# Twelve bf16 products of constants per chunk in the recurrence of a four-layer kernel

## The chip, the cores and the metric

The kernel runs on one core of one Trainium2 chip. The metric is the device time of one execution in microseconds (us). Lower is better.

## The reference, cut to what matters

The reference is a network of four layers, each an attention-like part plus a feed-forward part. The part that matters here is the attention of the first layer: a recurrence over time in which a memory matrix M is updated by each token and then normalised over all its entries.

```python
def step(M, kv):
    k_t, v_t = kv
    v_pred = jnp.einsum('bf,bfd->bd', k_t, M)
    surprise = jnp.linalg.norm(v_t - v_pred, axis=-1, keepdims=True)
    delta = k_t[:, :, None] * v_t[:, None, :]
    M = M + eta_c[None, :, None] * surprise[:, :, None] * delta
    return (_ln2(M), None)
M, _ = jax.lax.scan(step, M0, (kT, vT))
```

`_ln2` subtracts the mean of M and divides by its standard deviation. As the kernel lays it out there are 16 sequences of 256 tokens. The recurrence is serial in time: the scalar weight of each token depends on the state after the token before.

## The kernel before, in words

All engines have instruction streams written out by hand, and semaphores tie them together. The kernel is a row of stages with a barrier after each. The recurrence is the fourth stage. It works in chunks of C = 8 tokens; NC = 32 chunks, numbered c = 0 to 31.

Within a chunk the eight tokens are stepped through on VectorE (DVE) and ScalarE (ACT) alone, with small vectors: two square roots a step on ACT and some seven small operations on DVE. TensorE (PE) works at the border of two chunks and in the background. Its order for one chunk c is fixed by `scan_pe`:

- **The head.** Products of the new weights `vw` and `wc` with the masked key products of `cross_pe` (into PSUM banks 1 and 2); then, each waiting for a DVE addition (`sc_pT`), the product of `pT0` with the values (bank 5), the second part of `pT1`, four one-column sums (bank 3), and the product of `pT1` (bank 6). Then `rescale_pe`, whose result ACT copies (`sc_rc`) before it scales five of the eight blocks of the state (`scaled_act`), and only then takes the first square root of the chunk. Then PE waits for `sc_ex` and makes the **spreading product** `K("blk")` times `ex` (bank 7), from which DVE starts the steps.
- **The update.** `update_pe` makes 16 products with 32 rows each, `sums_pe` adds the scaled state through the identity in four pairs, waiting for ACT's scaling (`sc_scl`).
- **The keys.** `cross_pe` makes two products for chunk c + 2, of 256 columns each.
- **The state's products with the next keys.** Eight products of a block of the state with 16 tokens each (32 columns, fp32) into bank 4, in four pairs. Each pair waits for ACT's copy of two new blocks (`sc_new`), and ACT makes one copy in each of the steps 3 to 6. After them the next chunk's head waits for `vw` (`sc_vw`).

PE runs its stream strictly in order. A product of fp32 operands appears in the trace as two MATMUL records, one of bf16 operands as one. Every matrix product is recorded at the one line of the helper `mm`, L204; the tiles tell them apart:

- `ps<-big,tmp`, `ps<-big,sm`, `ps<-big,mw`: the head's wide products
- `ps<-co,mw` and `ps<-sm,co`: the one-column sums, and the rescaling product (8 columns)
- `ps<-mw,co` with 96 columns: the spreading product
- `ps<-tmp,big` and `ps<-sm,mw` with 32 rows: the update
- `ps<-big,co`: `sums_pe`
- `ps<-ke` and `ps<-ke,co`: `cross_pe`
- `ps<-ke,big` with 32 columns: the state's products with the next keys

On ACT, `sm<-ps 128x8` is the copy behind the rescaling product, `big<-big,co,sm` is `scaled_act`, `big<-ps 128x256` is the copy of new state blocks (and of bank 4 for the next chunk), and `sm<-sm 128x1` is a square root.

Of the kernel before, what the change touches and what calls it, by code (L numbers as in the profile page):

```python
# [12 lines left out]
BF16 = mybir.dt.bfloat16  # L13
# [119 lines left out]
def program(nc, xT, early, wts, bia, con, m1, m2, m3, outT):  # L133
    with ExitStack() as ctx:
# [13 lines left out]
        def signals(engine, *counts):  # L148
            out = []
            for n in counts:  # L150
                s, base = idle[engine].pop(0) if idle[engine] else (sem(f"{engine}_{next(made)}"), 0)
                out.append(Signal(s, base))
                held.append((engine, s, base + n))
            return out
# [16 lines left out]
        PS = ctx.enter_context(nc.psum_tensor("ps", [128, 8, 512], F32))  # L171

        def W(n, a=0, b=None):
            if n in EAT:
                o, w = EAT[n]
                return MW[:, 2048 + o + a:2048 + o + (w if b is None else b)]
            o, w = WAT[n]
            return WT[:, o + a:o + (w if b is None else b)]
# [5 lines left out]
        def K(n, a=0, b=None):  # L184
            if n in EAT:
                return W(n, a, b)
            o, w = CAT[n]
            return CO[:, o + a:o + (w if b is None else b)]
# [3 lines left out]
        def small(n):  # L192
            a = smat[0]
            smat[0] += n
            assert smat[0] <= 680
            return SM[:, a:a + n]
# [6 lines left out]
        def mm(e, out, lhsT, rhs, start=True, stop=True):  # L203
            return e.matmul(out, lhsT, rhs, start=start, stop=stop)  # L204
# [341 lines left out]
        def cv(buf, c):  # L546
            return buf[:, 128 * c:128 * c + 128]
# [163 lines left out]
        def tables_sp(e):  # L711
# [25 lines left out]
        C2 = small(16).rearrange("p (t x) -> p t x", x=2)  # L737
        one8r = small(8)
        rp8, Rc, Wst, tmp8 = small(8), small(8), small(8), small(8)
        corr = PS[:, 4, 0:256].rearrange("p (k n) -> p k n", k=2)  # L740
        ORDER = (0, 2, 4, 6, 1, 3, 5, 7)
        s_rt = [sem(f"d_rt{i}") for i in range(RTB)]
# [2 lines left out]
        sc_cross, sc_next, sc_p0, sc_p0e, sc_p1, sc_p2, sc_p3, sc_exp, sc_rc, sc_up, sc_sum = signals(  # L745
            "tensor", 31, 30, 31, 31, 31, 31, 31, 31, 32, 256, 124)
# [6 lines left out]
        def tok(c, a=0, b=128):  # L753
            return KE[:, :, 128 * c + a:128 * c + b]

        def cross_pe(e, c):
            if c > 1:
                e.wait_ge(*sc_xm(c - 1))
            mm(e, PS[:, 0, 0:256], cv(EK, c - 1), tok(c))
            mm(e, PS[:, 0, 256:512], K("one"), tok(c)).then_inc(sc_cross.sem, 1)  # L760
# [4 lines left out]
        def rescale_pe(e, c):  # L765
            e.wait_ge(*sc_rp(c))
            mm(e, PS[:, 4, 256:264], K("rselA"), rp8).then_inc(sc_rc.sem, 1)

        def update_pe(e, c):
            if c > 1:  # L770
                e.wait_ge(*sc_new(4 * (c - 1)))
            e.wait_ge(*sc_vwr(c))
            if c == 1:
                e.wait_ge(s_ek, 16 * 32)
            for mean in range(2):
                for a in ORDER:

                    r32 = slice(32 * (a // 2), 32 * (a // 2) + 32)
                    if mean:
                        mm(e, moved(a), K("hm", 128 * (a % 2), 128 * (a % 2) + 128)[r32, :], wcr[r32, :].broadcast_to((32, 128)),  # L780
                           start=False, stop=(c == NC and a % 2 == 1)).then_inc(sc_up.sem, 1)
                    else:
                        mm(e, moved(a), EK4[c - 1][r32, a % 2, :], vwr[r32, :], start=(a % 2 == 0), stop=False)

        def sums_pe(e, c):

            for k in range(4):
                e.wait_ge(*sc_scl(8 * (c - 1) + 2 * k + 2))
                mm(e, PS[:, (2, 3, 5, 6)[k], 0:256], K("ident"), U[:, 256 * k:256 * k + 256], start=False, stop=True).then_inc(sc_sum.sem, 1)

        def scan_pe(e):
            cross_pe(e, 1)
            for c in range(NC):
                if c:
                    e.wait_ge(*sc_vw(c))
                    e.wait_ge(*sc_xm(c))
                    mm(e, PS[:, 1, 0:128], vw, XMK[c % 2][:, 0:128], start=True, stop=False)
                    e.wait_ge(*sc_wc(c))
                    mm(e, PS[:, 1, 0:128], wc.broadcast_to((128, 128)), XMK[c % 2][:, 256:384], start=False, stop=True).then_inc(sc_p0.sem, 1)
                    mm(e, PS[:, 2, 256:384], vw, XMK[c % 2][:, 128:256], start=True, stop=False)  # L800
                    e.wait_ge(*sc_pT(2 * c - 1))
                    mm(e, PS[:, 5, 0:128], pT0, cv(VT, c)).then_inc(sc_p1.sem, 1)
                    mm(e, PS[:, 2, 256:384], wc.broadcast_to((128, 128)), XMK[c % 2][:, 384:512], start=False, stop=True).then_inc(sc_p0e.sem, 1)
                    mm(e, PS[:, 3, 257:258], pT0, K("one")[:, 0:1])
                    e.wait_ge(*sc_sq(c))
                    mm(e, PS[:, 3, 256:257], sqp, K("one")[:, 0:1]).then_inc(sc_p2.sem, 1)
                    e.wait_ge(*sc_pT(2 * c))
                    mm(e, PS[:, 6, 0:128], pT1, cv(VT, c)).then_inc(sc_p3.sem, 1)
                    rescale_pe(e, c)
                    e.wait_ge(*sc_ex(c))  # L810
                    mm(e, PS[:, 7, 0:96], K("blk"), ex).then_inc(sc_exp.sem, 1)
                    update_pe(e, c)
                    sums_pe(e, c)
                if c + 2 < NC:
                    cross_pe(e, c + 2)
                if c and c + 1 < NC:
                    for a in range(8):
                        if a % 2 == 0:
                            e.wait_ge(*sc_new(4 * (c - 1) + a // 2 + 1))
                        p = mm(e, corr[:, :, 16 * a:16 * a + 16], Mst[:, a, :], tok(c + 1, 16 * a, 16 * a + 16), start=(a == 0), stop=(a == 7))  # L820
                    p.then_inc(sc_next.sem, 1)
            rescale_pe(e, NC)
            update_pe(e, NC)

# [1985 lines left out]
        def _(e):  # L2810
# [7 lines left out]
            first_pe(e)  # L2818
            barrier(e, st.up())
            scan_pe(e)  # L2820
            barrier(e, st.up())
            mo_pe(e)
# [302 lines left out]
```

## Time and profile before

| | |
|---|---|
| median of 3 runs | 2213.94 us (2213.69 to 2222.31) |
| span of the profiled execution | 2256.3 us |
| PE busy | 1912.8 us (85%) |
| DVE busy | 1357.7 us (60%) |
| ACT busy | 1044.8 us (46%) |
| mean granted TensorE clock | 0.821 |
| recurrence's chunks in the trace | from 242 to 770 us |

The time is that of executions without the profiler; the span is from the first to the last instruction of one profiled execution, and no separate time is given for that one. In the profile, the granted clock is 1.00 at TensorE's full 2.4 GHz and 0.50 at 1.2 GHz. PE's busy time is high partly because a slow clock stretches its products. The columns of a timeline are: start, duration from the first start to the last end of a merged group, engine, line, operation, tiles, shape, count, and idle time before it with its releaser.

### The profile page before, as it was taken

The page shows a single profiled execution, that of the slowest core. Times are in us where ns is not written, and L with a number is a line of the kernel's source. Part 1 is how long each engine was busy: PE and PEld are TensorE (multiplying, and loading weights), DVE is VectorE, ACT ScalarE, POOL GpSimd, SP SyncE. Part 2 cuts the span into 40 slices and gives each one's busy share as a digit, 9 for nine tenths or more (in the row PEclk, how much of TensorE's full clock was granted, in tenths as well). Part 3 has the DMA queues.
Part 4 walks back from the last instruction along what each step waited for, and adds up shares of the span by engine and source line. Part 5 has one row for each costly group of instructions (what it writes and reads, how often), then busy time and mean ns, then how long its engine had stood idle before and what let it go on. Part 6 is the DMA issues. An engine that isn't in the chain of part 4 may idle for free.

```text
span 2256.3 us, 35340 instructions
## 1 busy us (share of the span) xinstructions
PE 1912.8 (85%) x12022; PEld 1293.6 (57%) x12022; DVE 1357.7 (60%) x4960; ACT 1044.8 (46%) x2490; POOL 319.3 (14%) x455
## 2 busy tenths in 40 slices
PE   6887777787778799999999888888899954999888
PEld 4464566666666566886555776555454542973333
DVE  3777888888888644676333485542121431569886
ACT  2433555665566423333444223454344313437667
POOL 0001000000000000330000002003126023406642
PEclk9999666667676568898999657998999967988989
DMA  2001100000000000000001100003013200635662
GB/s 111 1 13 36 32 22 22 19 19 25 19 19 19 34 1 1 2 3 2 0 1 75 40 1 1 1 15 97 13 12 50 89 14 30 113 69 91 98 103 40
DMA packets 93282, 76.09 MB, mean 34 GB/s; under 512 B 22320, under 2 KB 85168, under 8 KB 92336
## 3 DMA queue, kind: packets, MB, share of 16 engines
q1 hardware_dynamic: 85424, 65.31, 12.8%
q0 software_dynamic: 7680, 8.53, 2.0%
q8 instruction: 97, 1.59, 0.3%
q14 instruction: 81, 0.66, 0.1%
HBM read 48.86 MB, written 23.51 MB: 32 GB/s over the span
## 4 chain that ended last, share of the span: by engine, by line
PE 56%; DVE 23%; ACT 6%; DMA 4%; issue 4%; SPq 3%; another core or an unknown queue 1%; POOL 1%; DVEq 0%; PEld 0%; PEldq 0%; ACTq 0%; POOLq 0%
PE ps L204 52%; DVE sm L225 8%; ACT big L213 3%; DVE mw L225 3%; DMA d_pt<-big 3%; DVE big L217 2%; PE ps L208 2%; PE ps L2465 2%; SPq L2552 1%; DVE big L231 1%; DVE tmp L221 1%; ACT sm L213 1%; SPq L866 1%; DVE big L225 1%
## 5 line engine op out<-in xcount | busy, mean ns | idle before, releaser
L213 ACT ACTIVATE tmp<-ps,bi 128x512 f32<-128x512 f32 (+1 forms) x226 | 153.9, 684 | 200.8 <-PE ps L204 189.3
L204 PE MATMUL ps<-big,mw 128*128 128x512 f32 (+3 forms) x476 | 236.3, 593 | 11.6 <-DVEq L252 5.6
L213 ACT ACTIVATE sm<-sm 128x1 f32<-128x1 f32 x512 | 174.4, 341 | 106.6 <-DVE sm L225 96.0
L204 PE MATMUL ps<-ke,big 32*128 32x128 f32 (+2 forms) x1632 | 154.0, 296 | 62.3 <-ACT big L212 61.8
L204 PE MATMUL ps<-big,co 128*128 128x256 f32 (+1 forms) x360 | 180.5, 636 | 27.9 <-DMA bi<-bia 12.2
L213 ACT ACTIVATE big<-ps,co 128x512 f32<-128x512 f32 (+1 forms) x296 | 174.5, 648 | 61.3 <-PE ps L204 58.2
L204 PEld LDWEIGHTS ps<-ke,big 32*128 32x128 f32 (+2 forms) x1632 | 132.3, 195 | 87.4 <-ACT big L212 72.0
L231 DVE TENSOR_REDUCE big<-ps 128x2 f32<-128x512 f32 x256 | 161.2, 675 | 21.0 <-PE ps L204 20.7
L204 PE MATMUL ps<-ke 48*128 48x256 bf16 (+4 forms) x638 | 127.5, 315 | 34.7 <-DVE big L217 16.7
L204 PE MATMUL ps<-big,tmp 128*32 128x256 f32 (+2 forms) x1180 | 137.5, 424 | 22.9 <-DVE tmp L221 17.6
L217 POOL TENSOR_TENSOR big<-big,co 128x512 f32<-128x512 f32 x32 | 40.1, 1274 | 765.6 <-ACT big L212 765.6
L204 PE MATMUL ps<-tmp,mw 128*128 128x512 f32 x288 | 140.9, 601 | 0.7 <-ACT tmp L212 0.7
L204 PE MATMUL ps<-big 128*32 128x128 f32 (+5 forms) x898 | 130.1, 299 | 10.3 <-DMA big<-big 5.1
L204 PE MATMUL ps<-big,wt 128*128 128x512 f32 x208 | 114.5, 653 | 24.8 <-DVEq L252 14.4
L204 PEld LDWEIGHTS ps<-big,co 128*128 128x128 f32 x360 | 88.9, 276 | 75.8 <-issue 27.1
L204 PEld LDWEIGHTS ps<-co,sm 128*128 128x128 f32 (+1 forms) x708 | 95.2, 208 | 64.4 <-DVE sm L333 37.6
L212 ACT ACTIVATE big<-ps 128x256 f32<-128x256 f32 (+4 forms) x244 | 90.7, 381 | 89.2 <-PE ps L204 72.6
L204 PEld LDWEIGHTS ps<-big,mw 128*128 128x128 f32 (+1 forms) x476 | 93.0, 229 | 66.5 <-issue 36.8
L204 PE MATMUL ps<-co,sm 128*128 128x128 f32 (+1 forms) x708 | 109.1, 304 | 22.6 <-DVE sm L333 12.6
L204 PEld LDWEIGHTS ps<-ke 128*128 128x128 f32 (+3 forms) x638 | 65.9, 133 | 92.4 <-DVE big L217 23.5
L225 DVE SCALAR_TENSOR_TENSOR sm<-sm,mw 128x1 f32<-128x1 f32 (+1 forms) x480 | 101.0, 221 | 23.3 <-ACT sm L213 13.0
L204 PE MATMUL ps<-tmp,wt 128*128 128x512 f32 (+1 forms) x212 | 102.5, 574 | 11.6 <-issue 5.8
(254 smaller groups left out, 3834.5 us busy)
## 6 DMA issues: line engine op xcount, KB each, us to landing
mw<-d_tab SPq DMA_DIRECT2D x32, 328.0 KB, 3.4
mw<-m SPq DMA_DIRECT2D x2, 4096.0 KB, 12.7
d_pt<-big SPq DMA_DIRECT2D x32, 192.0 KB
ke<-d_pt SPq DMA_DIRECT2D x72, 64.0 KB
big<-d_pt SPq DMA_DIRECT2D x72, 64.0 KB
mw<-d_pt SPq DMA_DIRECT2D x48, 64.0 KB
d_xs<-big SPq DMA_DIRECT2D x1, 2560.0 KB, 15.3
big<-d_xs SPq DMA_DIRECT2D x5, 512.0 KB, 6.4
```

The lines of the kernel that those rows point to most:

```text
L204: return e.matmul(out, lhsT, rhs, start=start, stop=stop)
L208: return e.transpose(out, a, K("ident")[0:n, 0:n])
L212: return e.activation(out, in_, f, scale=scale, **kw)
L213: return e.activation(out, in_, f, bias=K("zero")[0:out.shape[0], :] if bias is None else bias, scale=scale, **kw)
L217: return e.tensor_tensor(out, a, b, op)
L221: return e.tensor_scalar(out, a, s1, None, op0)
L225: return e.scalar_tensor_tensor(out=out, in0=a, scalar=s, in1=b, op0=op0, op1=op1)
L231: return e.tensor_reduce(out, a, AX, op)
L866: e.dma_start(BIG[2 + hh][q, :].rearrange("p (c x) -> p c x", x=256)[:, :, 64 * (b % 4):64 * (b % 4) + 64], EKT[q, 16 * hh:16 * hh + 16, : ...
L2465: p = e.matmul(o, TMP[:, 2 + i % 2, 128 * j:128 * j + 128], MW[:, bass.ds(x * 512 + (4096 + 128 * j), 128)], start=False, stop=(j == 3))
L2552: e.dma_start(st_[j][r0 + 8 * t:r0 + 8 * t + 8], d_pt[n, j, part].rearrange("(h d) n -> d h n", d=8)).then_inc(s_st[n % 4], 16)
```

## The change

PE gets products of two constants, 128 rows by 128 columns of weights and 384 moving columns, in bf16 (a bit view of the constant table `colr`). Their results go to columns 128 to 511 of PSUM bank 1, which nobody reads. `heat_pe(e, n)` makes n of them. Two stand after the rescaling product, ahead of the wait for `sc_ex` and the spreading product, in chunks 1 to 31. Ten stand among the state's products with the next keys, in chunks 1 to 30: three behind each of the first three pairs, one behind the last. The signal `sc_next` is given by the last state product, as before, ahead of the one added product.

```diff
+        heat_w, heat_x = K("colr", 0, 64).bitcast(BF16), K("colr", 0, 192).bitcast(BF16)
...
+        def heat_pe(e, n):
+            for _ in range(n):
+                mm(e, PS[:, 1, 128:512], heat_w, heat_x)
...
                     rescale_pe(e, c)
+                    heat_pe(e, 2)
                     e.wait_ge(*sc_ex(c))
                     mm(e, PS[:, 7, 0:96], K("blk"), ex).then_inc(sc_exp.sem, 1)
...
                         p = mm(e, corr[:, :, 16 * a:16 * a + 16], Mst[:, a, :], tok(c + 1, 16 * a, 16 * a + 16), start=(a == 0), stop=(a == 7))
-                    p.then_inc(sc_next.sem, 1)
+                        if a == 7:
+                            p.then_inc(sc_next.sem, 1)
+                        if a % 2:
+                            heat_pe(e, 1 if a == 7 else 3)
```

## Rows read from the trace of the kernel before

**Rows 1.** The page, part 2: 40 equal slices of the span, in tenths.
```profile
PEclk9999666667676568898999657998999967988989
```

**Rows 2.** Windows: the recurrence, then the head of chunk 2 and later stretches.
```profile
core 0: us, PE busy (x) PEld busy (x) DVE busy (x) ACT busy (x) POOL busy (x), PEclk, DMA share, GB/s
242.00:770.00 528.00, 418.65 (x2436) 346.19 (x2436) 454.18 (x2749) 319.18 (x949) 0.00 (x0) 0.67 0.06 19
250.80:254.60 3.80, 2.60 (x18) 2.23 (x18) 3.56 (x25) 1.21 (x4) 0.00 (x0) 1.00 0.30 91
492.60:497.00 4.40, 4.34 (x18) 3.99 (x18) 3.45 (x22) 0.79 (x3) 0.00 (x0) 0.50 0.23 76
497.70:503.80 6.10, 5.99 (x41) 4.51 (x42) 5.42 (x32) 4.87 (x15) 0.00 (x0) 0.50 0.00 1
506.00:510.00 4.00, 1.89 (x12) 1.56 (x12) 3.40 (x24) 2.65 (x10) 0.00 (x0) 1.00 0.00 0
```

**Rows 3.** Waits of PE from 267 to 752 us: in total, times, longest, us.
```profile
PE ps L204 <- ACT big L212: 60.1, 85, 0.8
...
PE ps L204 <- ACT big L213: 6.2, 10, 1.0
```

**Rows 4.** The chain in order of time, heads of chunks 3 and 16: start, us, what.
```profile
267.03 4.34 PE ps L204 x18
...
492.64 4.35 PE ps L204 x18
497.02 0.19 ACT sm L212
497.23 2.04 ACT big L213 x5
```

**Rows 5.** Timeline of PE, chunk 2: first and last product of its head, and behind.
```profile
250.83 0.49 PE L204 MATMUL ps<-big,tmp 128*128 128x128 f32 x2 [0.37 <-DVE tmp L221]
...
253.69 0.29 PE L204 MATMUL ps<-sm,co 128*128 128x8 f32 x2
254.95 0.74 PE L204 MATMUL ps<-mw,co 128*128 128x96 f32 x2 [0.97 <-DVE mw L217]
```

**Rows 6.** Timeline of ACT, heads of chunks 2 and 16.
```profile
254.01 0.18 ACT L212 ACTIVATE sm<-ps 128x8 f32<-128x8 f32 x1 [1.47 <-PE ps L204]
...
256.16 0.28 ACT L213 ACTIVATE sm<-sm 128x1 f32<-128x1 f32 x1
...
499.17 0.28 ACT L213 ACTIVATE sm<-sm 128x1 f32<-128x1 f32 x1
```

**Rows 7.** Timeline of PE, the last head (chunk 31); of ACT, its first square root.
```profile
752.36 0.79 PE L204 MATMUL ps<-big,tmp 128*128 128x128 f32 x2
...
757.47 0.74 PE L204 MATMUL ps<-mw,co 128*128 128x96 f32 x2 [0.78 <-DVE mw L217]
...
758.88 0.28 ACT L213 ACTIVATE sm<-sm 128x1 f32<-128x1 f32 x1
```

**Rows 8.** Timeline of PE, the last layers: bf16 products of 256 columns and their neighbours.
```profile
1414.60 1.87 PE L204 MATMUL ps<-ke 128*128 128x256 bf16 x8
1416.26 1.91 PE L204 MATMUL ps<-co,sm 128*128 128x128 f32 x8
...
1419.10 1.03 PE L204 MATMUL ps<-ke 128*128 128x256 bf16 x8
1420.01 1.16 PE L204 MATMUL ps<-co,sm 128*128 128x128 f32 x8
```

**Rows 9.** Timeline of PEld and PE, the state's products with the next keys.
```profile
490.12 0.89 PEld L204 LDWEIGHTS ps<-ke,big 128*128 128x128 f32 x4 [0.88 <-ACT big L212]
...
508.92 0.52 PEld L204 LDWEIGHTS ps<-ke,big 128*128 128x128 f32 x4 [0.88 <-ACT big L212]
...
508.93 0.63 PE L204 MATMUL ps<-ke,big 128*128 128x32 f32 x4 [0.77 <-ACT big L212]
510.04 0.49 PE L204 MATMUL ps<-big,tmp 128*128 128x128 f32 x2 [0.48 <-DVE tmp L221]
```

## Prediction

> **What bounds the kernel now.** I read the page first, then windows over the recurrence, then PE's waits, then the chain and the timelines of single chunks. In the page the reader should look at the line of the granted clock: full in the first slices, then 0.6 to 0.7 for the ten slices of the recurrence [rows 1]. The windows give that stretch as 528 us, a quarter of the span, at a mean clock of 0.67 [rows 2]. DVE is busy 454 us of it and PE 419, but neither is full: the chunk is one serial chain that changes engines. What matters is where PE stands on this chain, and at which clock.
>
> PE is off the chain while the eight tokens are stepped. It then waits for ACT's copies, 85 times for 60.1 us in all, and no wait is longer than 1.0 us [rows 3]. During the state's products with the next keys it is busy 1.89 of 4.00 us, at the full clock; behind that stretch the clock falls, and the head of chunk 16, where PE is busy 4.34 of 4.40 us, runs at 0.50 [rows 2]. So does the stretch after it (5.99 of 6.10 us), and the clock comes back only then. PE is slow where the chain goes through it, and fast where it waits.
>
> In the head PE is on the chain: 4.35 us of products in chunk 16, then ACT's copy of the rescaling factors, 2.04 us of scaling, and the first square root [rows 4]. The scaling on ACT, not the spreading product, ends last there, so what counts is how early the rescaling product comes.
>
> **What a head is worth at the full clock.** The trace has the case once. The head of chunk 2 ran at 1.00 up to its spreading product [rows 2]. From its first product (250.83) to the end of the rescaling product (253.69 and 0.29) it took 3.15 us, against 4.35 us in chunk 16; ACT's copy came at 254.01, 3.18 us after the first product, against 4.38 (492.64 to 497.02); the first square root at 256.16, 5.33 against 6.53 (492.64 to 499.17) [rows 4, 5, 6]. So a head at the full clock is 1.20 us shorter. The whole chunk confirms it: 250.83 to 267.03 is 16.20 us. The next 28, from 267.03 to 752.36 [rows 4, 7], take 485.33 us, 17.33 each. Some of these already have the first products of the head at full clock, which is why the mean is 17.33 and not 17.40.
>
> If every head ran like that of chunk 2: 28 x 16.20 = 453.6, so 31.7 us less; and the head of chunk 31, from 752.36 to its square root at 758.88, is 6.52 us instead of 5.33 [rows 6, 7], 1.2 us more. Sum 32.9 us. The head of chunk 1 gains nothing, since the update behind it waited for a transfer.
>
> **What the added products cost.** No row has one of 384 columns. The nearest are bf16 products of 128 rows and 256 columns: eight take 0.91 us at the full clock (1419.10 to 1420.01), 0.114 each, and eight take 1.66 us at, nearly all, half of it (1414.60 to 1416.26), 0.21 each [rows 8]. Times 1.5: 0.17 and 0.31 us each. Per chunk that is 2.0 us or 3.7 us of PE. Whether it costs anything depends on the waits:
>
> - Between the state's products. The waits of some 0.77 us lie between pairs 1.40 us apart, one for each step. At full clock a pair keeps the array's loads busy 0.52 us [rows 9], and three added products 0.51: 1.03 of 1.40 us, hidden. The last pair starts 1.11 us ahead of the next head (508.93 to 510.04 [rows 9]): 0.52 + 0.17 leaves 0.4 us. Cost 0. The cover is gone at half clock: 0.89 + 0.93 = 1.82 of 1.40 us, and the fourth pair then ends with 3 x 1.82 + 0.89 + 0.31 = 6.66 us after the first began, where the head is due after 4.20 + 1.11 = 5.31. The head would come 1.35 us late.
> - Before the spreading product. PE waits 0.78 us at half clock and 0.97 at full [rows 5, 7], two added products take 0.62 or 0.34. Cost 0 in both, with 0.16 us to spare at half clock.
> - Moved: `sc_next` is still given by the last state product, so ACT's copy of bank 4 is not later. No wait and no DMA is added. 362 products in all, written where nothing is read, in a bank whose only reader (the addition for `pT0`) is past when they run.
>
> **Does the clock hold?** This is what the change hangs on, and rows bear it out only in part. In the stretch where the clock was lost PE worked 1.89 of 4.00 us; the ten products add about 1.7 us, most of them there, which makes some 3.3 of 4. Behind the keys and in the head of chunk 2 the clock was at 1.00 with PE busy 2.60 of 3.80 us [rows 2], and that head now gets two products more. So the busy share with the change is above that of the one head that was fast. Against it: in chunk 2 the clock had fallen by 255 us, right behind the head, and the wait ahead of the spreading product is the longest idle piece left. A fall there is nearly free, since the update and the sums are not on the chain, and these dense stretches brought the clock back in every chunk.
>
> On such gaps the Trainium skill has two statements that pull apart. Its page "TensorE: Matmul & The Clock Gate", table "Why this matters for your kernels", warns only of long idle gaps between bursts of products, longer than any here; by that rule the clock would not be lost in this stretch at all, and the change could give nothing. The trace disagrees, with falls where the longest wait is 1.0 us [rows 3]. The same page, "A second HAM failure mode", says that frequent micro-idles between groups of products are enough to make the clock swing between its two levels; by that rule filling them gives the 32.9 us above. The trace agrees with this one (full, then 0.50 [rows 2]).
>
> I take it that the clock holds in five heads of six: with chunks getting shorter, a fall will at times land at the end of the state's products, where the last pair has only one added product and PE then waits for `vw`. 32.9 x 5/6 = 27.4 us. The span is 2256.3 us against a median of 2213.94, 1.9% more; taking 27.4 as 1.9% less changes half a us, so I leave it. 2213.94 - 27.4 = 2186.5, **2187 us**.
>
> **The rivals.**
>
> 1. *The clock holds only in part.* It stays up through the state's products but falls in half of the heads or more, because the head has three waits for DVE and only the last of them is filled. Then 32.9 x 1/2 or less is gained: 2197 to 2209 us. For it: the falls so far come anywhere around the head. Against it: chunk 2.
> 2. *The products cost more than they return* (the other side). If the added columns do not count as work enough and the clock stays at 0.50 from one head into the next state's products, each step overruns and the head comes 1.35 us late [rows 9]: 30 x 1.35 = 40 us, up to 2254 us; with half of the chunks so, 2234. It decides from the point where the clock is at half for more than one pair, for one overrun of 0.42 us is taken up by the 0.4 us ahead of the head. For it: the clock comes back late in some chunks. Against it: before the change it was back by the second pair in the chunks I looked at.
> 3. *Nothing changes.* The falls stay where they are, or the added work fills waits only. 2214 us, 2209 to 2218. It is what the page's rule on long gaps says; the rows speak against it.
>
> **How the numbers follow.** Chances: the forecast (gain 15 to 33 us or a little more, 2178 to 2199) 0.70; rival 1 0.11; rival 2 0.10; rival 3 0.09. 0.5% is 11 us, about what a measurement of this kernel can tell from no change. Below 2202.9: the forecast and half of rival 1, 0.76. Within: the other half of rival 1 and rival 3, less a little, 0.14. Above 2225: 0.10. The lower end of the range is the full 32.9 us and 3 more for chunk 2's own tail and later stages, 2178; the upper end goes through rival 1, 2209. The forecast's own range is 2178 to 2199.
>
> **What would show it.** In windows over the recurrence, the mean clock rises from 0.67 to 0.85 or more; chunks are 16.2 us apart; ACT's copy comes about 3.2 us after the head's first product; the wait for ACT's copies shrinks from 0.77 to about 0.3 us; the step's rhythm on ACT stays 1.40 us. I am wrong if PE stops waiting for ACT's copies at all (rival 2), or if heads still take 6.5 us to the first square root (rivals 1 and 3).

## The result, and the profile after

The changed kernel takes 2183.86 us (median of 4 runs, 2181.05 to 2198.83), the kernel before 2214.28 us (4 runs). The ratio is 0.9871, with a 95% interval of 0.9844 to 0.9899: 1.3% faster. The forecast was 2187 us, with a range of 2178 to 2209.

The spans of the two profiles, 2256.3 and 2184.8 us, differ by 72 us, far more than the runs do. 44 us of that lie after 1400 us, in the layers that wait for transfers, which the change does not touch. From that instruction (1400.0 us in the kernel before) to the end, the ten profiles of this document took 812 to 819 us in five and 850 to 871 us in the other five. That goes with the chip and not with the kernel: the four experiments run on chip 7, where the kernel before has a median of 2212.99 us, are all among the short ones, and the four run on chip 9, where it has 2253.12 us, all among the long ones; for the two profiles of this section the chip is not on record. What lies ahead of the recurrence varies as well: the head of chunk 1 starts at 233.2 to 238.7 us. So I compare stretches of the recurrence, not spans. The profile of the kernel with 8 columns is of a slow execution (2277.52 us, where its other ten took 2238 to 2255).

The page after, part 2, 40 slices of the span, granted clock in tenths; the counterpart is [rows 1]:

```profile
PEclk9999688899888779898999756898999978989989
```

Windows of the kernel after; columns as in [rows 2]:

```profile
242.00:770.00 528.00, 417.30 (x2874) 306.24 (x2874) 456.90 (x2788) 323.42 (x969) 0.00 (x0) 0.85 0.08 23
464.60:469.80 5.20, 4.06 (x27) 2.43 (x26) 4.51 (x31) 3.49 (x12) 0.00 (x0) 1.00 0.00 0
469.80:474.00 4.20, 3.02 (x21) 2.36 (x21) 3.92 (x27) 1.61 (x6) 0.00 (x0) 1.00 0.26 80
```

The first line is the stretch of the recurrence: its clock went from 0.67 to 0.85 while PE's busy time stayed at some 417 us. PE did more work in the same time. The next two are one chunk: the state's products, where PE is now busy 4.06 of 5.20 us, and the head behind them, which runs at 1.00.

The timeline of PE over the same chunk, for which [rows 5, 9] were the counterparts:

```profile
464.61 0.53 PE L204 MATMUL ps<-ke,big 128*128 128x32 f32 x4
464.97 0.65 PE L204 MATMUL ps<-co 128*128 128x384 bf16 x3
465.89 0.63 PE L204 MATMUL ps<-ke,big 128*128 128x32 f32 x4 [0.27 <-ACT big L212]
466.36 0.65 PE L204 MATMUL ps<-co 128*128 128x384 bf16 x3
467.29 0.63 PE L204 MATMUL ps<-ke,big 128*128 128x32 f32 x4 [0.28 <-ACT big L212]
...
469.16 0.33 PE L204 MATMUL ps<-co 128*128 128x384 bf16 x1
469.81 0.49 PE L204 MATMUL ps<-big,tmp 128*128 128x128 f32 x2 [0.32 <-DVE tmp L221]
...
472.67 0.29 PE L204 MATMUL ps<-sm,co 128*128 128x8 f32 x2
472.81 0.48 PE L204 MATMUL ps<-co 128*128 128x384 bf16 x2
473.92 0.46 PE L204 MATMUL ps<-mw,co 128*128 128x96 f32 x2 [0.63 <-DVE mw L217]
```

The waits in brackets shrank from 0.77 to 0.27 us, but did not vanish: the pairs still start 1.40 us apart (465.89 to 467.29), and the head still starts when `vw` is ready. The products are free here. From the head's first product (469.81) to the end of the rescaling product (472.96) it is 3.15 us.

The chain in order of time for that head; its counterpart is the chain in [rows 4]:

```profile
472.01 0.29 DVE mw L217
...
472.34 0.63 PE ps L204 x4
...
472.99 0.19 ACT sm L212
...
473.20 2.03 ACT big L213 x5
475.24 0.19 ACT sm L213
```

Where PE held the chain for 4.35 us, it holds it for 0.63 us now. The rest of the head is DVE's own small operations, which a faster TensorE does not shorten. That is why the head gained 1.2 us and not half of 4.35.

I read the start of each head (the first `ps<-big,tmp`) and the first square root after it, for all chunks. Heads 2 and 31 start at 254.74 and 733.03, so 29 chunks take 478.3 us; before it was 752.36 less 250.83, 501.5 us. Of the heads of chunks 3 to 31, 23 take 5.33 to 5.34 us to their first square root, and six do not: 6.52, 6.36, 6.52, 6.36, 6.52 and 5.85 us in chunks 5, 9, 10, 25, 29 and 31. Two chunks are long for another reason: in chunks 8 and 24 the next head starts 11.94 and 12.00 us after the first square root, where it is 10.93 and 10.87 in their neighbours (chunk 30 is 0.4 us late). Here is chunk 8, first in the timeline of PE:

```profile
358.64 1.89 PE L204 MATMUL ps<-big,co 128*128 128x256 f32 x6
362.63 0.70 PE L204 MATMUL ps<-big,co 128*128 128x256 f32 x2 [2.10 <-ACT big L213]
...
364.33 0.90 PE L204 MATMUL ps<-ke,big 128*128 128x32 f32 x4
365.05 1.15 PE L204 MATMUL ps<-co 128*128 128x384 bf16 x3
365.99 0.90 PE L204 MATMUL ps<-ke,big 128*128 128x32 f32 x4
...
370.01 0.51 PE L204 MATMUL ps<-co 128*128 128x384 bf16 x1
370.31 0.63 PE L204 MATMUL ps<-big,tmp 128*128 128x128 f32 x2
```

and in windows:

```profile
359.60:363.60 4.00, 1.84 (x7) 1.17 (x7) 3.78 (x24) 2.92 (x10) 0.00 (x0) 1.00 0.00 0
364.00:370.00 6.00, 6.00 (x27) 4.90 (x26) 5.19 (x35) 3.49 (x11) 0.00 (x0) 0.50 0.01 1
370.00:374.60 4.60, 4.60 (x21) 4.19 (x22) 2.86 (x18) 0.87 (x3) 0.00 (x0) 0.50 0.26 73
```

PE waits 2.10 us ahead of the fourth sum, and is busy 1.84 of 4.00 us around it. The clock falls right behind. Pairs and added products then take 1.66 us a step (364.33 to 365.99) instead of 1.40, PE has no wait left, the head comes 1.0 us late (11.94 against 10.93), and it (chunk 9) runs at half clock as well. Behind that head PE is just as busy, and the clock is still at half:

```profile
374.60:380.70 6.10, 5.97 (x42) 4.15 (x40) 5.39 (x30) 4.98 (x15) 0.00 (x0) 0.50 0.00 0
```

### The profile page after: what moved, and what is told of

It reads as the page before. It is cut to its first block, busy times and chain, and to the rows that moved or that the text cites. A ratio compares the mean times of both kernels' runs of the same rounds, so it can differ in the third digit from the quotient of the medians.

```text
span 2184.8 us, 36064 instructions
## 1 busy us (share of the span) xinstructions
PE 1877.0 (86%) x12384; PEld 1236.7 (57%) x12384; DVE 1348.9 (62%) x4960; ACT 1041.5 (48%) x2490; POOL 319.4 (15%) x455
## 4 chain that ended last, share of the span: by engine, by line
PE 55%; DVE 26%; ACT 6%; issue 4%; DMA 4%; SPq 3%; POOL 1%; DVEq 0%; PEld 0%; PEldq 0%; ACTq 0%; POOLq 0%
PE ps L204 51%; DVE sm L225 8%; ACT big L213 3%; DVE mw L225 3%; DVE big L217 3%; DMA d_pt<-big 2%; PE ps L208 2%; DVE big L231 2%; PE ps L2474 2%; SPq L2561 1%; DVE tmp L221 1%; DVE sm L221 1%; ACT sm L213 1%; SPq L875 1%; DVE big L225 1%
## 5 line engine op out<-in xcount | busy, mean ns | idle before, releaser
L204 PE MATMUL ps<-big,mw 128*128 128x512 f32 (+3 forms) x476 | 220.2, 555 | 23.0 <-DVE mw L217 9.6
L204 PE MATMUL ps<-big,co 128*128 128x256 f32 (+1 forms) x360 | 159.7, 560 | 65.5 <-ACT big L213 44.1
L204 PEld LDWEIGHTS ps<-ke,big 32*128 32x128 f32 (+2 forms) x1632 | 137.3, 196 | 56.4 <-ACT big L212 36.2
L204 PE MATMUL ps<-big,tmp 128*32 128x256 f32 (+2 forms) x1180 | 125.4, 407 | 21.6 <-DVE tmp L221 17.1
L204 PEld LDWEIGHTS ps<-big,co 128*128 128x128 f32 x360 | 71.2, 227 | 108.1 <-ACT big L213 66.9
L204 PEld LDWEIGHTS ps<-big,mw 128*128 128x128 f32 (+1 forms) x476 | 81.8, 201 | 77.1 <-issue 35.4
L204 PE MATMUL ps<-big,wt 128*128 128x512 f32 x208 | 109.0, 625 | 16.8 <-DVEq L252 14.3
L204 PEld LDWEIGHTS ps<-ke 128*128 128x128 f32 (+3 forms) x638 | 67.0, 135 | 83.5 <-DVE big L217 23.2
L213 ACT ACTIVATE big<-big,co,sm 128x128 f32<-128x128 f32 x248 | 107.5, 480 | 1.0
```

The lines of the kernel that those rows point to most:

```text
L213: return e.activation(out, in_, f, bias=K("zero")[0:out.shape[0], :] if bias is None else bias, scale=scale, **kw)
```

## The experiments

All timed against the kernel before on the same chip: chip 9 for the ten alone, the two alone, 8 columns and four ahead of the sum, chip 7 for the others below the change. The table gives the results in the order of the text; the times of 29 chunks are from the heads of chunk 2 to 31 in each profile, the clock is the mean over 257 to 736 us, "slow heads" are those of chunks 3 to 31 that take over 5.6 us.

| kernel | ratio | 95% interval | 29 chunks, us | clock | slow heads |
|---|---|---|---|---|---|
| before | 1 | | 501.5 | 0.68 | 29 |
| the change | 0.9871 | 0.9844 to 0.9899 | 478.3 | 0.86 | 6 |
| ten, without the two | 0.9895 | 0.9849 to 0.9941 | 475.8 | 0.84 | 4 |
| the two alone | 0.9988 | 0.9966 to 1.0009 | 501.0 | 0.69 | 29 |
| 8 columns | 0.9985 | 0.9964 to 1.0006 | 500.5 | 0.67 | 29 |
| 192 columns | 0.9994 | 0.9964 to 1.0023 | 498.0 | 0.70 | 29 |
| six a step | 1.0001 | 0.9978 to 1.0025 | 496.1 | 0.90 | 0 |
| four ahead of the sum | 0.9903 | 0.9878 to 0.9928 | 474.5 | 0.95 | 6 |
| the change again | 0.9892 | 0.9844 to 0.9941 | 478.0 | 0.86 | 4 |
| all holes | 0.9855 | 0.9823 to 0.9887 | 470.7 | 0.95 | 1 |

None of the added products is part of what the reference computes; no kernel here leaves anything of it out.

**The ten products without the two ahead of the spreading product.**

```diff
-                    heat_pe(e, 2)
                     e.wait_ge(*sc_ex(c))
```

> The ten products among the state's products alone, without the two ahead of the spreading product. Theory (the clock is lost in the waits between the state's products and carried from there into the head; the two in the head's own wait matter little): the gain stays, ratio to the kernel before 0.985 to 0.990, mean clock over the recurrence above 0.80, most heads 5.3 us from their first product to the first square root. Rival (the head's waits have to be filled too, or the clock is lost there on the chain): half of the gain or less, ratio 0.993 or more, heads of 6.3 to 6.5 us in most chunks.

The ratio is 0.9895, at the edge of what was expected, and its interval reaches past the rival's 0.993. The trace decides: 475.8 us for the 29 chunks, 2.5 us less than with the change, and 25 of 29 heads under 5.6 us, where the rival wanted 6.3 to 6.5 in most. Its four slow heads are as many as in the second profile of the change. The two products ahead of the spreading product are not needed. This refutes the rival, and with it a part of my own prediction, which counted on them for the head.

**The two alone.**

```diff
-                        if a % 2:
-                            heat_pe(e, 1 if a == 7 else 3)
```

> The two products ahead of the spreading product alone. Theory: nothing is carried into the head, so nothing is gained: ratio 0.998 to 1.002, clock over the recurrence 0.67 to 0.70. It measures the cost of the two at half clock too: 0.62 us of products in a wait of 0.78, so none. Rival (the two cost time at half clock): ratio above 1.002, the spreading product more than 5.12 us behind the head's first product.

As expected: no gain, and no cost either, since the spreading product still comes 5.11 to 5.12 us behind the first product in heads at half clock.

**The same twelve, 8 columns wide.**

```diff
-                mm(e, PS[:, 1, 128:512], heat_w, heat_x)
+                mm(e, PS[:, 1, 128:136], heat_w, heat_x[:, 0:8])
```

> All twelve products in their places, but with 8 moving columns instead of 384: same count of instructions and weight loads, almost no streaming. Theory (the clock follows the work that the array does, so the width makes the gain): ratio 0.998 to 1.003, clock 0.67 to 0.70, heads as before. Rival (that PE is never idle for long, or has instructions and weight loads in its queue, keeps the clock): ratio 0.985 to 0.992, clock above 0.80.

The timeline of PE in one chunk of it, the last two pairs and the first products of the head:

```profile
455.72 0.63 PE L204 MATMUL ps<-ke,big 128*128 128x32 f32 x4 [0.71 <-ACT big L212]
456.19 0.22 PE L204 MATMUL ps<-co 128*128 128x8 bf16 x3
457.12 0.63 PE L204 MATMUL ps<-ke,big 128*128 128x32 f32 x4 [0.71 <-ACT big L212]
...
458.79 0.63 PE L204 MATMUL ps<-big,tmp 128*128 128x128 f32 x2
459.58 0.79 PE L204 MATMUL ps<-big,mw 128*128 128x128 f32 x2 [0.15 <-DVE mw L217]
```

The products are there, but the head slows down in its third product as it did before. In this kernel it is the width of the added products that makes the gain, not their instructions or weight loads in the queue.

**The same twelve, 192 columns wide.**

```diff
-                mm(e, PS[:, 1, 128:512], heat_w, heat_x)
+                mm(e, PS[:, 1, 128:320], heat_w, heat_x[:, 0:192])
```

> The twelve products in their places with 192 moving columns, half of the work. Theory (there is a need of array work in the waits, and the changed kernel meets it with little to spare): most of the gain is lost, ratio 0.994 to 1.000, clock over the recurrence 0.67 to 0.75. Rival (any work in the waits will do, in proportion): half the gain, ratio 0.992 to 0.994, clock 0.76.

Half of the work gives 3.5 us in the chunks instead of 23.2, and no gain that the runs can tell (0.9994). The most frequent head is 6.25 us: the clock is held some tenths of a us into the head, then lost. At 8, 192 and 384 columns the chunks gain 1.0, 3.5 and 23.2 us, so the rival of a gain in proportion is out.

**Six products a step.**

```diff
-                            heat_pe(e, 1 if a == 7 else 3)
+                            heat_pe(e, 2 if a == 7 else 6)
```

> Twice the products among the state's products: six behind each of the first three pairs and two behind the last, two ahead of the spreading product. Theory (the added products are free only as long as they fit between two pairs): at full clock a pair and six products take 0.52 + 6 x 0.17 = 1.5 us of the step's 1.40, and the next head comes some 0.3 us late; where the clock is at half it comes over 3 us late. The stretch from the first square root to the next head grows from 10.87 to 11.1 us or more in every chunk, the gain shrinks to ratio 0.990 to 1.000, with the clock over the recurrence above 0.80. Rival (more work is always better, since it holds the clock and PE is off the chain there): ratio below 0.987.

The gain is gone in the runs (1.0001, just outside what was expected), with the highest clock so far in the recurrence, 0.90. Its timeline of PE:

```profile
458.38 0.53 PE L204 MATMUL ps<-ke,big 128*128 128x32 f32 x4
458.74 1.14 PE L204 MATMUL ps<-co 128*128 128x384 bf16 x6
459.72 0.53 PE L204 MATMUL ps<-ke,big 128*128 128x32 f32 x4
...
461.42 0.49 PE L204 MATMUL ps<-co 128*128 128x384 bf16 x2
461.75 0.38 PE L204 MATMUL ps<-big,tmp 128*128 128x128 f32 x2
```

The verdict was right and its size at full clock wrong: a step takes 1.34 us (458.38 to 459.72), not 1.5, so it fits into 1.40. But there is no slack left: what PE falls behind where the clock is at half (in this kernel it falls ahead of the fourth sum in nearly every chunk, and is back in the middle of the pairs) cannot be made good, and each head comes 12.05 us after the square root instead of 10.87. Every head runs at full clock, and a head that starts late takes only 4.98 us, since it waits less for DVE: 1.5 us less than the 6.52 of before, for a start 1.2 us late. That leaves 0.3 us a chunk, 5.4 us in 29, and chunk 1 loses 2.5 of them (20.17 us from head to head, where it was 17.64); what is left is too little for the runs to tell.

**Four more ahead of the fourth sum, and two behind the last pair.**

```diff
+                if k == 3:
+                    heat_pe(e, 4)
                 e.wait_ge(*sc_scl(8 * (c - 1) + 2 * k + 2))
...
-                            heat_pe(e, 1 if a == 7 else 3)
+                            heat_pe(e, 2 if a == 7 else 3)
```

> As the change, and four more products ahead of the fourth of the sums (where PE waits for ACT's scaling) and one more behind the last pair. Theory: the chunks in which the changed kernel still lost time are those where the clock fell during the sums (and was back only in the middle of the state's products, whose added work then overran) or at the end of the state's products; both holes are filled, all heads take 5.3 us and all chunks 16.2: 3 to 6 us less than the change, ratio to the kernel before 0.983 to 0.986. Rival (the falls that are left have another cause, or the added work delays the keys): ratio 0.987 or more.

The ratio missed (0.9903, on the rival's side), and so did "all heads take 5.3 us": six were still slow, at 5.7 to 6.1 us, and ahead of five of them the clock had fallen 0.6 to 1.2 us before the head. The sum of the chunks did not miss: 474.5 us, 3.8 less than with the change. Up to 1369 us of its trace it is 30.8 us ahead of the kernel before, the change 27.4, and from there both it and the kernel before take 856 us. The medians on its chip are only 24.0 us apart (2253.12 and 2229.10); where the rest went is not known. The runs alone could not have told this kernel and the change apart.

**The change again, and all holes filled.**

```diff
+                if k == 3:
+                    heat_pe(e, 5)
                 e.wait_ge(*sc_scl(8 * (c - 1) + 2 * k + 2))
...
-                            heat_pe(e, 1 if a == 7 else 3)
+                            heat_pe(e, (3, 3, 4, 2)[a // 2])
```

> The changed kernel itself, beside the others on one chip: ratio 0.986 to 0.990, 29 chunks in 476 to 480 us, and the stage behind the recurrence about 5 us shorter than in the kernel before, as in its first profile. Rival for that stage: the 5 us were chance, and it takes what it took before.

> As the change, with five products ahead of the fourth sum, and 3, 3, 4 and 2 behind the four pairs (the change has 3, 3, 3, 1). The falls left with four ahead of the sum and 3, 3, 3, 2 came 0.6 to 1.2 us ahead of a head, so the stretch ahead of them gets one product more. Theory: no head is left above 5.4 us, 29 chunks take 29 x 16.2 = 470 to 471 us against 478 with the change, ratio to the kernel before 0.982 to 0.986. Rival (the falls move elsewhere, or the added work overruns): 474 us or more.

The change repeats itself: 478.0 us, ratio 0.9892. With all holes filled the 29 chunks take 470.7 us, 16.23 each, where chunk 2 of the kernel before took 16.20. Two heads are above 5.4 us (5.68 and 5.53), where none was expected. Windows over 257 to 736 us, first the change, then all holes filled:

```profile
257.00:736.00 479.00, 384.63 (x2664) 283.80 (x2664) 425.45 (x2611) 301.18 (x899) 0.00 (x0) 0.86 0.07 20
```

```profile
257.00:736.00 479.00, 396.26 (x2933) 276.17 (x2931) 430.36 (x2649) 305.61 (x914) 0.00 (x0) 0.95 0.07 21
```

It is the fastest kernel of this study, at 0.9855 of the kernel before and a median of 2182.34 us against 2190.90 of the change on the same chip. The intervals of the two overlap, so the 7 us between them rest on the traces.

## Why the prediction was right, point by point

- **What a head is worth at full clock: right.** Taken from chunk 2, 5.33 against 6.53 us; 23 heads now take 5.33 or 5.34, and the copy on ACT comes 3.18 us after the first product.
- **The added products' cost: right in sign, too high in size.** Predicted 0.17 us each at full clock and 0.31 at half; measured 0.163 (six in 0.98 us, 458.74 to 459.72) and 0.313 (365.05 to 365.99). The pair was taken for the time of its loads, 0.52 and 0.89 us, and takes 0.36 (464.61 to 464.97) and 0.72. A step at half clock is 1.66 us, not 1.82, and the head comes 1.0 to 1.1 us late, not 1.35.
- **The clock holds in five heads of six: right, 23 of 29.** The share was a guess that the rows of before bounded but did not give.
- **The two products in the head: wrong as a reason.** "That head now gets two products more" was an argument for holding the clock. Without them the clock held in 25 heads.
- **"The wait ahead of the spreading product is the longest idle piece left": wrong.** This is the one step that failed. A faster PE is done with three sums early and waits 2.10 us for ACT's scaling ahead of the fourth; in 267 to 752 us before, waits of this kind were 6.2 us in all and 1.0 at most [rows 3], in 257 to 736 us after they are 42.0 us and 2.2. In eight chunks the clock fell about there (9.2 to 10.2 us after the head's first product), came back 3.4 us later and cost nothing. In chunks 8 and 24 it fell at 10.7 and 10.6 us and came back only behind the next head. Rival 2's mechanism is real: the added work overran and took 2.1 us in these two chunks, and heads 9 and 25 behind them were 1.0 us slow each. Filling the hole (four and five products) removed it, and doubling the products between the pairs made it the rule.
- **"A fall there is nearly free": right for a fall behind the head, of which it was said.** In chunks 3, 12, 13, 16, 20 and 27 the clock fell 3.9 to 4.8 us after the head's first product, and the next head started on time and took 5.33 or 5.34 us. Windows from chunk 16 show one, at half clock up to 496.8 us; its next head starts at 502.19:

```profile
490.10:496.80 6.70, 6.69 (x43) 5.17 (x44) 6.07 (x36) 5.26 (x16) 0.00 (x0) 0.50 0.01 4
496.90:502.10 5.20, 4.47 (x30) 3.06 (x29) 4.51 (x30) 3.49 (x12) 0.00 (x0) 1.00 0.00 0
```

- **Falls at the end of the state's products: right.** Heads 5 and 29 (6.52 us) are slow because the clock fell 0.8 us ahead of them, in the last pair. For head 5, which starts at 303.04:

```profile
298.20:302.20 4.00, 3.17 (x22) 1.81 (x21) 3.53 (x22) 2.79 (x9) 0.00 (x0) 1.00 0.00 0
302.30:309.10 6.80, 6.65 (x30) 5.11 (x33) 5.44 (x32) 2.71 (x8) 0.00 (x0) 0.50 0.17 49
```

The other two slow heads lost it as head 10 began, and 4.1 us ahead of head 31.
- **The sum.** The prediction put 27.4 us into the recurrence. The 29 chunks gave 23.2 and the last head 0.7 (5.85 against 6.52), together 23.9; what fell short of 32.9 is mainly six slow heads (6.1 us) and the late ones (2.5 us). Chunk 1, which stands in neither count, took 1.0 us more (18.61 us from head to head, 17.64 before; 17.60 in the change again), so the recurrence as a whole gave 22.9. The rest came from a place to which the sum gave nothing, the stage behind the recurrence:

Windows over that stage, before and after:

```profile
769.60:834.30 64.70, 55.99 (x245) 36.52 (x246) 27.20 (x90) 13.65 (x35) 0.00 (x0) 0.61 0.08 29
```

```profile
749.60:809.00 59.40, 50.70 (x248) 31.53 (x248) 27.05 (x90) 13.50 (x35) 0.00 (x0) 0.69 0.09 32
```

The same work takes 5.3 us less, since the clock comes back some 11 us earlier in it. The same 59.3 to 59.5 us stand in the profiles of the change again, of the ten alone, and of both kernels with products ahead of the sum; the kernels with 8 and 192 columns have 64.7, the two alone 61.7 and six a step 61.6. So it goes with the gain and not with chance alone, but why the clock comes back earlier there was not tried and stays open. 22.9 and 5.3 are 28.2 us, against 30.4 between the medians. That 27.4 came so close is in part luck: the recurrence gave 4.5 us less than that, and a stage outside the sum made up for it.

The two statements on the Trainium skill's page "TensorE: Matmul & The Clock Gate" came out as weighed. The warning about long gaps in its table "Why this matters for your kernels" does not cover this kernel: with waits of at most 1.0 us [rows 3] the clock was lost in all 29 heads before. Its section "A second HAM failure mode", that frequent micro-idles are enough, is borne out: filling short waits held the clock in 23 of 29 heads after. The runs add that it matters what fills them: 8 columns shortened the waits from 0.77 to 0.71 us and changed nothing.

## What to carry to other kernels

When a serial chain passes through TensorE for a short time after it sat in short waits, look at the granted clock of that piece, not at its busy share, and look for one piece of the same work that ran at full clock: it prices the gain. Work that nobody reads is free only while it fits into the wait at half clock too, or the kernel never gets to half clock; so fill the holes evenly, count the slack, and look again after the change, because a faster engine opens a new hole elsewhere. Judge such a change by the stretch it acts on as well as by the runs, since stretches that it does not touch can differ by more from profile to profile (812 to 871 us here).

## What the runs showed of the hardware that was not expected

Half of the added columns held the clock in none of the 29 heads, and all of them in 23; no width between the two was tried. A PE that is busy does not always get its clock back: in chunk 8 it was busy 6.00 of 6.00 us at half clock, and 5.97 of 6.10 behind the next head, before the clock rose. And a bf16 product of 384 columns takes 0.163 us at full clock and 0.313 at half, nearly the ratio of the two clocks (1.92): in this order of products no weight load shows in their pace.
